# Router scores as 64 more columns of the z product, from a product of keys and Wq made once on the chip

## The chip, the cores and the metric

The kernel runs on one core of a Trainium2 chip. The metric is the device time of one execution in microseconds (us); the time before is 255.06 us, the median of three runs (254.93 to 255.38). The engines are TensorE (PE; its weight loads are PEld), VectorE (DVE), ScalarE (ACT), GpSimd (POOL) and SyncE (SP), which here issues nearly all transfers.

## The reference

For x of 32 x 64 x 1024, with J = 512 (64 experts of rank 8):

```
h    = conv1d(x, weight, 9 taps, 4 groups) + (cond @ c_weight.T)[:, :, None] + bias[None, :, None]
q    = h @ Wq.T                     # 1024 -> 16
s    = q @ keys.T                   # 16 -> 64 scores
gate = softmax over the 16 largest of s, 0 elsewhere
z    = (h @ A.T) gated, 8 columns for each expert      # 1024 -> 512
out  = x + 2 * (z @ B.T)            # 512 -> 1024
```

All is f32. A product of the kernel that has to be exact to nearly f32 is made from a rounded high half and a low half of each operand, in three passes: high x high, high x low, low x high. The halves have the type f32r (fp32r in the profile).

## The kernel before

The 2048 rows of 1024 are cut into 16 tiles (t or i) of 128 rows. A tile runs through these steps:

- **Convolution** (`conv`, L388): the tile's input, in blocks, is split by ScalarE (x_hi, `high` L253) and VectorE (x_lo, `low` L517); 2 groups of 6 matmuls of 512 columns each go to p_conv (tile 1: p_out). ScalarE adds the condition and the bias (`add_u`, L276, tile h_c), VectorE transposes in 32x32 blocks (`turn_h`, L534, h_t), and both split again (h_hi, h_lo).
- **z product** (`z_product`, L411): the stationary operand is a 128x128 chunk of h, the moving one a row block of A. A's 512 columns and Wq's 16 stand side by side in a_raw, a_hi and a_lo (JQ = 528) and are cut into two banks of HB = 264. So a tile has 8 chunks x 3 passes x 2 banks = 48 matmuls of 264 columns into p_z (tile 1: p_out). The last 16 columns of bank 1 are q.
- **Scores**: ScalarE copies q out (`take_q`, L306), TensorE turns it against the identity (`turn_q`, L422, f32, into p_q), ScalarE copies the turned q (`copy_q`, L310), TensorE multiplies it with the keys (`scores`, L426, a plain f32 matmul of 64 columns, two records in the profile), VectorE copies the scores (`copy_scores`, L559).
- **Gate**: VectorE finds the 16 largest (`choose`), ScalarE takes the exponential, VectorE makes e_top and the reciprocal of its sum (`weigh`, L582) and gates z (`gate`, L594, z_g, which frees the banks of p_z).
- **Output**: TensorE turns z_g (`turn_z`, L433, p_t), both engines split it (zt_hi, zt_lo), 24 matmuls of 512 columns make z @ B (`out_part`, L450 to L452), and VectorE adds x (`add`, L605). The last tile's second half is cut into two parts of 256 columns.

Every engine's order is written out by hand, and each engine runs its own in order; semaphores join them. TensorE's order: conditioning (4 matmuls, L460), convolutions of tiles 0 to 2, z of tile 0, convolution 3 (with turn_q(0) between its groups, scores(0) behind it), z of tile 1, z of tile 2 in pieces with the scores of 1 and 2 and turn_z(0) between them, convolution 4, turn_z(1), output of tile 0. From tile 3 on: z(i), with turn_q(i) in the middle of the second pass of bank 0, scores(i), convolution i+2, turn_z(i-1), output of tile i-2. Bank 1 comes before bank 0. The first z product of a tile waits for the gate of the tile before (L399 to L401).

At the start, ScalarE splits w and x of tiles 0 and 1, adds for tile 0, splits x of tile 2 and h of tile 0, and then the six chunks of A that are its own (a_hi; VectorE rounds chunks 5 and 7, L547, and makes every a_lo). ScalarE's queue issues one load, sm (conditioning, bias and keys); SyncE's queue has w, x of tiles 0 to 2, A, x of tile 3, B and the rest, in that order. GpSimd makes the constants, and later one x_lo, that of tile 4 (L247).

Of the kernel before, what the change touches and what calls it, by code (L numbers as in the profile page):

```python
# [6 lines left out]
ACT = mybir.ActivationFunctionType  # L7
# [3 lines left out]
P = 128  # L11
# [14 lines left out]
RD = 16  # L26
JQ = J + RD
HB = JQ // 2
E = 64
RANK = 8  # L30
JC = J // P
D = 128
SMALL_CW, SMALL_C, SMALL_B, SMALL_K = 0, 64, 96, 100
SMALL = 164


def adaln_ffn(nc, x_blocks, x_rows, conv_w, a_wq, b_w, small, out):

# [9 lines left out]
    with ExitStack() as ctx:  # L48
        def sb(name, shape, dt=F32):
            return ctx.enter_context(nc.sbuf_tensor(name, shape, dt))  # L50
# [4 lines left out]
        def sem(name):  # L55
            return ctx.enter_context(nc.semaphore(name))
# [14 lines left out]
        h_lo = sb("h_lo", [P, 2, R, P], F32R)  # L71
        a_raw = sb("a_raw", [P, R, JQ])
        a_hi = sb("a_hi", [P, R, JQ], F32R)
        a_lo = sb("a_lo", [P, R, JQ], F32R)
        b_raw = sb("b_raw", [P, JC, L])
# [7 lines left out]
        zt_lo = sb("zt_lo", [P, 2, JC, P], F32R)  # L83
        q_s = sb("q_s", [P, P])
        q_t = sb("q_t", [P, P])
        sc = sb("sc", [P, E])
# [14 lines left out]
        p_q = ps("p_q", [P, 512])  # L101
        QT, SC = slice(0, P), slice(P, P + E)

# [30 lines left out]
        s_z = sem("s_z")  # L134
        s_q = sem("s_q")
        s_qz = sem("s_qz")
        s_ahd = sem("s_ahd")
        s_qtp = sem("s_qtp")
        s_qt = sem("s_qt")
        s_scp = sem("s_scp")  # L140
        s_nm = sem("s_nm")
# [47 lines left out]
        @block.sync  # L189
        def _(sp):  # L190
            def load_blocks(t):
                if t >= XB:
                    sp.wait_ge(s_xhi, x_split_count(t - XB))
                    sp.wait_ge(*x_lo_done(t - XB))
                sp.dma_start(x_blk[:, t % XB], x_blocks[t]).then_inc(s_xb[t % XB], 16)

            def load_rows(t):
                if t >= XN:
                    sp.wait_ge(s_st[t % XN], 32 * (t // XN))
                sp.dma_start(x_nat[:, t % XN, :], x_rows[t]).then_inc(s_xn[t % XN], 16)  # L200
# [12 lines left out]
            for r in range(R):  # L213
                sp.dma_start(a_raw[:, r, :], a_wq[:, r]).then_inc(s_a[r], 16)
            load_blocks(3)
            for c in range(JC):
                sp.dma_start(b_raw[:, c, :], b_w[:, c]).then_inc(s_b[c], 16)
            load_blocks(4)
            sp.dma_start(w_raw[:, 1], conv_w[:, 1]).then_inc(s_w[1], 16)
            for t in range(XN):  # L220
                load_rows(t)
            for i in range(2, NT):
                if i + 3 < NT:
                    load_blocks(i + 3)
                store(i - 2)
                if 1 <= i - 2 and i + 1 < NT:
                    load_rows(i + 1)
            store(NT - 2)
            store(NT - 1)
            for k in range(XN):  # L230
                last = NT - XN + k
                sp.wait_ge(s_st[k], 32 * (last // XN) + 16 * len(parts(last)))

        @block.gpsimd
        def _(pool):
            nc.gpsimd.memset(ones[:], 1.0).then_inc(s_ones, 1)
            nc.gpsimd.memset(ident[:], 0.0).then_inc(s_iz, 1)
            nc.gpsimd.memset(q_s[:], 0.0).then_inc(s_qz, 1)
            pool.wait_ge(s_iz, 1)
# [11 lines left out]
        def _(act):  # L251
# [34 lines left out]
            def split_a(r):  # L286
                act.wait_ge(s_a[r], 16)
                high(a_hi[:, r, :], a_raw[:, r, :], s_ahi)

# [9 lines left out]

            def take_q(i):  # L300
                act.wait_ge(s_zq, i + 1)
                if i == 0:
                    act.wait_ge(s_qz, 1)
                if i >= 1:
                    act.wait_ge(s_qtp, i)
                nc.scalar.activation(q_s[:, 0:RD], z_bank(i, 1)[:, J - HB:HB], ACT.Copy).then_inc(s_q, 1)  # L306

            def copy_q(i):
                act.wait_ge(s_qtp, i + 1)
                nc.scalar.activation(q_t[:], p_q[:, QT], ACT.Copy).then_inc(s_qt, 1)  # L310

# [3 lines left out]

            act.dma_start(sm[:], small).then_inc(s_small, 16)
            split_w(0)
            split_x(0, 0)
# [5 lines left out]
            split_x(2)  # L324
            split_h(0)
            for r in A_ACT:
                split_a(r)
# [4 lines left out]
            add_u(2, 1)  # L332
            take_q(0)
            copy_q(0)
            split_h(1)
# [5 lines left out]
            split_h(2)  # L341
            take_q(1)
            split_b(1)
            copy_q(1)
            split_b(2)
            split_b(3)
            take_q(2)
            exp(1)
            split_z(0)
            copy_q(2)  # L350
            for i in range(2, NT):
                if i == 2:
                    split_h(3)
                else:
                    take_q(i)
                    copy_q(i)
                exp(i)
# [13 lines left out]
        def _(pe):  # L371
# [20 lines left out]
            def z_product(t, k, banks, chunks):  # L392
# [12 lines left out]
                for r in chunks:  # L405
                    if t == 0 and k == 0:
                        pe.wait_ge(*a_hi_done(r))
                    if t == 0 and k == 2:
                        pe.wait_ge(s_alo, r + 1)
                    for b in banks:  # L410
                        mm = nc.tensor.matmul(z_bank(t, b)[:, 0:HB], h[:, t % 2, r, :], a[:, r, b * HB:(b + 1) * HB],  # L411
                                              start=k == 0 and r == 0, stop=k == 2 and r == R - 1)
                        if k == 2 and r == R - 1:
                            mm.then_inc(s_zq if b else s_z, 1)

            def turn_q(i):
                pe.wait_ge(s_q, i + 1)
                if i >= 1:
                    pe.wait_ge(s_dve, STEPS * (i - 1) + 1)
                else:  # L420
                    pe.wait_ge(s_ident, 1)
                nc.tensor.transpose(p_q[:, QT], q_s[:], ident[:]).then_inc(s_qtp, 1)  # L422

            def scores(i):
                pe.wait_ge(s_qt, i + 1)
                nc.tensor.matmul(p_q[:, SC], q_t[:], sm[:, SMALL_K:SMALL_K + E], start=True, stop=True).then_inc(s_scp, 1)  # L426

# [35 lines left out]
            mm.then_inc(s_up, 1)  # L463
            for t in range(3):
                for g in range(NG):
                    conv(t, g)
            for k in range(3):
                z_product(0, k, (1, 0), range(R))
            conv(3, 0)
            turn_q(0)  # L470
            conv(3, 1)
            scores(0)
            for k in range(3):
                z_product(1, k, (1, 0), range(R))
            z_product(2, 0, (1,), range(R))
            turn_q(1)
            z_product(2, 1, (1,), range(R))
            scores(1)
            z_product(2, 2, (1,), range(R))
            turn_z(0)  # L480
            z_product(2, 0, (0,), range(R))
            z_product(2, 1, (0,), range(R // 2))
            turn_q(2)
            z_product(2, 1, (0,), range(R // 2, R))
            z_product(2, 2, (0,), range(R))
            scores(2)
            for g in range(NG):
# [4 lines left out]
            for i in range(3, NT):  # L492
# [3 lines left out]
                z_product(i, 1, (0,), range(R // 2))  # L496
                turn_q(i)
                z_product(i, 1, (0,), range(R // 2, R))
                z_product(i, 2, (0,), range(R))
                scores(i)  # L500
                if i + 2 < NT:
# [13 lines left out]
        def _(dve):  # L515
# [25 lines left out]
            def split_a(r):  # L541
                dve.wait_ge(*a_hi_done(r))
                low(a_lo[:, r, :], a_raw[:, r, :], a_hi[:, r, :], s_alo)

            def round_a(r):
                dve.wait_ge(s_a[r], 16)
                nc.vector.tensor_copy(a_hi[:, r, :], a_raw[:, r, :]).then_inc(s_ahd, 1)  # L547

# [8 lines left out]
            def copy_scores(i):  # L557
                dve.wait_ge(s_scp, i + 1)
                nc.vector.tensor_copy(sc[:], p_q[:, SC]).then_inc(s_dve, 1)  # L559

# [58 lines left out]
            split_x(2)  # L619
            split_h(0)  # L620
            split_a(0)
            round_a(5)
# [54 lines left out]
def laid_out(x, cond, bias, conv_w, cond_w, A_w, B_w, Wq_w, keys):  # L677
# [20 lines left out]

    a = np.concatenate([chunked(A_w), chunked(Wq_w)], axis=2)
    b = B_w.T.reshape(JC, P, L).transpose(1, 0, 2)  # L700
# [4 lines left out]
    small[:, SMALL_B:SMALL_B + 2 * NG] = np.tile(bias.reshape(2 * NG, CI).T, (R, 1))  # L705
    small[0:RD, SMALL_K:SMALL_K + E] = keys.T
    return {"x_blocks": x_blocks, "x_rows": x_rows, "conv_w": w, "a_wq": a, "b_w": b, "small": small}

# [21 lines left out]
```

## Time and profile before

| | |
|---|---|
| median of three runs | 255.06 us |
| the profiled execution | 253.84 us, of it a span of 252.0 us |
| TensorE busy | 246.4 us, 98% of the span |
| VectorE, ScalarE, GpSimd busy | 56%, 39%, 2% |
| granted clock of TensorE | 1.00 over the span |

The span runs from the first to the last instruction in the trace; the time of an execution holds some 1.8 us more. A matmul's length in the trace overlaps the next one's, so what it occupies is read from the distance of the starts.

### The profile page before, as it was taken

How to read it: one execution, taken by the hardware profiler on the slowest of the kernel's cores; microseconds unless marked ns; L12 is line 12 of the kernel's file. 1: busy time of each engine (PE TensorE's matmuls, PEld its weight loads, DVE VectorE, ACT ScalarE, POOL GpSimd, SP SyncE). 2: the span in 40 equal slices, each digit the busy share in tenths (PEclk: the TensorE clock that was granted, in tenths of full speed). 3: DMA queues.
4: the chain of work that ended last, by engine and by line, in shares of the span. 5: the costliest groups of instructions: out<-in, count | busy, mean ns of one | idle time of the engine just before them, and what ended most of it. 6: DMA issues, size and time to landing. Idle time of an engine off the chain costs nothing.

```text
span 252.0 us, 3991 instructions
## 1 busy us (share of the span) xinstructions
PE 246.4 (98%) x1492; PEld 218.6 (87%) x1492; DVE 141.4 (56%) x339; ACT 98.4 (39%) x239; POOL 4.0 (2%) x10
## 2 busy tenths in 40 slices
PE   7999899999999999999999999999999999999995
PEld 7689898898989889898998989889898988989885
DVE  1796989969175572827539173562817546151622
ACT  5896853635081531606135080532606133101100
POOL 2000300000000000000000000000000000000000
PEclk9999999999999999999999999999999999999999
DMA  7999400051604215070331605115070401313122
GB/s 218 383 409 406 196 4 0 0 170 41 209 3 140 110 54 201 0 246 8 126 124 42 211 0 188 65 70 181 3 250 1 134 35 43 127 42 125 54 103 97
DMA packets 11828, 30.37 MB, mean 120 GB/s; under 512 B 1312, under 2 KB 1696, under 8 KB 11808
## 3 DMA queue, kind: packets, MB, share of 16 engines
q1 hardware_dynamic: 11664, 30.02, 33.3%
q8 instruction: 12, 0.20, 0.3%
q10 hardware_dynamic: 144, 0.08, 0.2%
q14 instruction: 8, 0.07, 0.1%
HBM read 21.71 MB, written 8.39 MB: 119 GB/s over the span
## 4 chain that ended last, share of the span: by engine, by line
PE 90%; DVE 3%; DMA 2%; ACT 2%; issue 1%; SPq 1%; DVEq 0%; ACTq 0%
PE p_z L411 35%; PE p_conv L388 15%; PE p_out L452 12%; PE p_out L451 12%; PE p_out L450 12%; PE p_t L433 3%; DMA x_blk<-in_x_blocks 2%; PE p_q L426 1%; ACT h_c L276 1%; PE p_q L422 1%; DVE e_top L582 1%; DVE x_lo L517 0%; DVE h_lo L517 0%; ACT h_hi L253 0%; ACT x_hi L253 0%
## 5 line engine op out<-in xcount | busy, mean ns | idle before, releaser
L450 PE MATMUL p_out<-b_hi,zt_hi 128*128 128x512 f32 (+1 forms) x128 | 51.2, 400 | 0.0
L452 PE MATMUL p_out<-b_hi,zt_lo 128*128 128x512 f32 (+1 forms) x128 | 50.4, 393 | 0.0
L451 PE MATMUL p_out<-b_lo,zt_hi 128*128 128x512 f32 (+1 forms) x128 | 50.1, 391 | 0.0
L559 DVE COPY sc<-p_q 128x64 f32<-128x64 f32 x16 | 3.6, 224 | 66.7 <-PE p_q L426 66.7
L276 ACT ACTIVATE h_c<-p_conv,u 128x128 f32<-128x128 f32 x120 | 33.9, 380 | 6.2 <-PE p_conv L388 6.2
L411 PE MATMUL p_z<-a_hi,h_lo 128*128 128x264 f32 x240 | 35.6, 289 | 0.0
L411 PE MATMUL p_z<-a_hi,h_hi 128*128 128x264 f32 x240 | 34.3, 286 | 0.9 <-DVE z_g L594 0.9
L411 PEld LDWEIGHTS p_z<-a_hi,h_hi 128*128 128x128 f32 x240 | 32.2, 188 | 2.3 <-issue 1.1
L411 PE MATMUL p_z<-a_lo,h_hi 128*128 128x264 f32 x240 | 34.1, 284 | 0.0
L411 PEld LDWEIGHTS p_z<-a_hi,h_lo 128*128 128x128 f32 x240 | 31.9, 189 | 0.0
L411 PEld LDWEIGHTS p_z<-a_lo,h_hi 128*128 128x128 f32 x240 | 31.3, 188 | 0.0
L452 PEld LDWEIGHTS p_out<-b_hi,zt_lo 128*128 128x128 f32 x128 | 24.0, 188 | 5.5
L451 PEld LDWEIGHTS p_out<-b_lo,zt_hi 128*128 128x128 f32 x128 | 24.1, 188 | 5.2
L450 PEld LDWEIGHTS p_out<-b_hi,zt_hi 128*128 128x128 f32 x128 | 24.1, 188 | 5.0
L605 DVE SCALAR_TENSOR_TENSOR x_nat<-p_out,x_nat 128x512 f32<-128x512 f32 (+1 forms) x32 | 21.7, 679 | 11.5 <-PE p_out L452 11.0
L306 ACT ACTIVATE q_s<-p_z 128x16 f32<-128x16 f32 x15 | 2.8, 184 | 64.5 <-PE p_z L411 64.5
L534 DVE STREAM_TRANSPOSE h_t<-h_c 128x512 f32<-128x512 f32 x32 | 22.4, 706 | 4.9 <-ACT h_c L276 4.9
L517 DVE TENSOR_TENSOR h_lo<-h_t,h_hi 128x1024 fp32r<-128x1024 f32 x16 | 19.6, 1224 | 8.8 <-ACT h_hi L253 8.8
L517 DVE TENSOR_TENSOR x_lo<-x_blk,x_hi 128x1032 fp32r<-128x1032 f32 (+1 forms) x17 | 18.7, 1100 | 6.3 <-ACT x_hi L253 6.3
L388 PE MATMUL p_conv<-x_hi,w_hi 128*128 128x512 f32 x60 | 20.2, 418 | 0.0
L253 ACT ACTIVATE h_hi<-h_t 128x1024 fp32r<-128x1024 f32 x16 | 17.0, 1064 | 7.7 <-DVE h_t L534 7.7
L388 PE MATMUL p_conv<-x_lo,w_hi 128*128 128x512 f32 x60 | 19.1, 400 | 0.5 <-DVE x_lo L517 0.5
(71 smaller groups left out, 238.5 us busy)
## 6 DMA issues: line engine op xcount, KB each, us to landing
x_nat<-in_x_rows SPq DMA_DIRECT2D x16, 512.0 KB, 4.0
out_dram<-x_nat SPq DMA_DIRECT2D x31, 256.0 KB, 2.1
x_blk<-in_x_blocks SPq DMA_DIRECT2D x14, 516.0 KB, 4.7
a_raw<-in_a_wq SPq DMA_DIRECT2D x8, 264.0 KB, 7.2
b_raw<-in_b_w SPq DMA_DIRECT2D x4, 512.0 KB, 9.8
x_blk<-in_x_blocks SPq DMA_DIRECT2D x4, 258.0 KB, 4.2
w_raw<-in_conv_w SPq DMA_DIRECT2D x2, 256.0 KB, 8.0
out_dram<-x_nat SPq DMA_DIRECT2D x2, 128.0 KB, 1.7
```

Of the source, the lines that this page charges most:

```text
L253: nc.scalar.activation(dst, src, ACT.Copy).then_inc(s, 1)
L276: last = nc.scalar.activation(h_c[:, t % 2, g, n, :], conv_bank(t, g)[:, n * LB:(n + 1) * LB], ACT.Identity, bias=u[:, t // 8 * NG + g, at ...
L388: mm = nc.tensor.matmul(bank, w[:, pair, s, g, :], x[:, t % 2, g, :, s:s + LB], start=k == 0 and s == 0, stop=k == 2 and s == 1)
L411: mm = nc.tensor.matmul(z_bank(t, b)[:, 0:HB], h[:, t % 2, r, :], a[:, r, b * HB:(b + 1) * HB], start=k == 0 and r == 0, stop=k == 2 and r ...
L433: mm = nc.tensor.transpose(p_t[:, c * P:(c + 1) * P], z_g[:, t % 2, c * P:(c + 1) * P], ident[:])
L450: nc.tensor.matmul(dst, zt_hi[:, t % 2, c, :], b_hi[:, c, cols], start=c == 0, stop=False)
L451: nc.tensor.matmul(dst, zt_hi[:, t % 2, c, :], b_lo[:, c, cols], start=False, stop=False)
L452: mm = nc.tensor.matmul(dst, zt_lo[:, t % 2, c, :], b_hi[:, c, cols], start=False, stop=c == JC - 1)
L517: nc.vector.tensor_tensor(dst, src, hi.bitcast(F32), ALU.subtract).then_inc(s, 1)
L534: nc.vector.transpose(h_rows[:, :, :, g, :], h_c[:, t % 2, g].rearrange("q n (k c) -> q n k c", c=CI)).then_inc(s_tr, 1)
L559: nc.vector.tensor_copy(sc[:], p_q[:, SC]).then_inc(s_dve, 1)
L605: nc.vector.scalar_tensor_tensor(out=x_nat[:, t % XN, lo:hi], in0=src, scalar=SCALING, in1=x_nat[:, t % XN, lo:hi], op0=ALU.mult, op1=ALU. ...
```

## The change

Wq and keys are joined on the chip, once: an own load brings wk (16 x 1088: Wq's columns in the order of A's chunks, then keys turned), and 8 plain f32 matmuls of 64 columns make keys x Wq, chunk by chunk, into p_q. ScalarE and VectorE split that as high and low halves into 64 more columns of a_hi and a_lo. The z product's columns grow from 528 to 576 (banks of 288), and its last 64 columns are the scores; the 16 for q are gone. `take_q`, `turn_q`, `copy_q` and `scores` are gone in every tile, and so are q_s, q_t and GpSimd's fill of q_s; `copy_scores` reads p_z once bank 1 is complete. TensorE makes the keys product between the convolutions of tiles 0 and 1; both splits stand ahead of the splits of A on their engines. a_raw has 512 columns.

```diff
-JQ = J + RD
-HB = JQ // 2
+JE = J + E
+HB = JE // 2
@@ ScalarE
-                high(a_hi[:, r, :], a_raw[:, r, :], s_ahi)
+                high(a_hi[:, r, 0:J], a_raw[:, r, :], s_ahi)
-            def take_q(i):
...
-            def copy_q(i):
...
+            def split_wk():
+                act.wait_ge(s_wkp, 1)
+                high(a_hi[:, :, J:JE], p_q[:].rearrange("p (r e) -> p r e", r=R), s_wkhi)
             act.dma_start(sm[:], small).then_inc(s_small, 16)
+            act.dma_start(wk[:], wq_keys).then_inc(s_wk, 16)
...
             split_h(0)
+            split_wk()
             for r in A_ACT:
                 split_a(r)
@@ TensorE
                     if t == 0 and k == 0:
                         pe.wait_ge(*a_hi_done(r))
+                    if t == 0 and k == 0 and r == 0:
+                        pe.wait_ge(s_wkhi, 1)
+                    if t == 0 and k == 2 and r == 0:
+                        pe.wait_ge(s_wklo, 1)
...
-            for t in range(3):
+            for g in range(NG):
+                conv(0, g)
+            pe.wait_ge(s_wk, 16)
+            for r in range(R):
+                mm = nc.tensor.matmul(p_q[:, r * E:(r + 1) * E], wk[:, r * P:(r + 1) * P], wk[:, L:L + E], start=True, stop=True)
+            mm.then_inc(s_wkp, 1)
+            for t in range(1, 3):
                 for g in range(NG):
                     conv(t, g)
...
                 z_product(i, 1, (0,), range(R // 2))
-                turn_q(i)
                 z_product(i, 1, (0,), range(R // 2, R))
                 z_product(i, 2, (0,), range(R))
-                scores(i)
@@ VectorE
+            def split_wk():
+                dve.wait_ge(s_wkhi, 1)
+                low(a_lo[:, :, J:JE], p_q[:].rearrange("p (r e) -> p r e", r=R), a_hi[:, :, J:JE], s_wklo)
             def copy_scores(i):
-                dve.wait_ge(s_scp, i + 1)
-                nc.vector.tensor_copy(sc[:], p_q[:, SC]).then_inc(s_dve, 1)
+                dve.wait_ge(s_zq, i + 1)
+                nc.vector.tensor_copy(sc[:], z_bank(i, 1)[:, J - HB:HB]).then_inc(s_dve, 1)
...
             split_h(0)
+            split_wk()
             split_a(0)
```

## Rows read from the trace of the kernel before

**Rows 1.** The page's first part: busy us (share of the span) x instructions.
```profile
PE 246.4 (98%) x1492; PEld 218.6 (87%) x1492; DVE 141.4 (56%) x339; ACT 98.4 (39%) x239; POOL 4.0 (2%) x10
```

**Rows 2.** The page's chain that ended last, by engine.
```profile
PE 90%; DVE 3%; DMA 2%; ACT 2%; issue 1%; SPq 1%; DVEq 0%; ACTq 0%
```

**Rows 3.** The waits of TensorE: us in total, times, longest.
```profile
PE p_z L411 <- DVE z_g L594: 0.9, 1, 0.9
...
PE p_conv L388 <- DVE x_lo L517: 0.5, 1, 0.5
```

**Rows 4.** Windows of PE: stretch, busy (matmuls), granted clock, DMA, GB/s.
```profile
15.50:21.35 5.85, 5.85 (x49) 1.00 1.02 405
...
107.63:116.64 9.01, 9.01 (x64) 1.00 0.50 173
...
107.63:122.67 15.04, 15.04 (x92) 1.00 0.31 107
246.31:249.07 2.76, 2.76 (x24) 1.00 0.25 95
```

**Rows 5.** PE in order of time (start, us, what), convolution of tile 3, first group.
```profile
21.36 0.64 PE L388 MATMUL p_conv<-x_hi,w_hi 128*128 128x512 f32 x2
...
22.78 0.27 PE L422 MATMUL p_q<-ident,q_s 128*128 128x128 f32 x1
```

**Rows 6.** PE in order of time, the last output matmuls.
```profile
238.16 0.40 PE L451 MATMUL p_out<-b_lo,zt_hi 128*128 128x512 f32 x1
...
246.32 0.28 PE L450 MATMUL p_out<-b_hi,zt_hi 128*128 128x256 f32 x1
```

**Rows 7.** PE in order of time, turn and scores of a steady tile.
```profile
112.03 0.27 PE L422 MATMUL p_q<-ident,q_s 128*128 128x128 f32 x1
112.06 0.74 PE L411 MATMUL p_z<-a_hi,h_lo 128*128 128x264 f32 x4
...
113.61 0.33 PE L426 MATMUL p_q<-sm,q_t 128*128 128x64 f32 x2
113.75 0.71 PE L388 MATMUL p_conv<-x_hi,w_hi 128*128 128x512 f32 x2
114.30 0.63 PE L388 MATMUL p_conv<-x_hi,w_lo 128*128 128x512 f32 x2
```

**Rows 8.** PE in order of time, the start.
```profile
5.14 1.08 PE L460 MATMUL p_t<-sm,cw 128*128 128x32 f32 x8 [0.52 <-POOL cw L243]
...
8.99 0.63 PE L388 MATMUL p_out<-x_hi,w_hi 128*128 128x512 f32 x2
...
11.81 0.71 PE L388 MATMUL p_conv<-x_hi,w_hi 128*128 128x512 f32 x2
```

**Rows 9.** DMA issues of the first 20 us: KB each, median us to landing.
```profile
sm<-in_small ACTq DMA_DIRECT2D x1, 82.0 KB, 3.7
```

**Rows 10.** Groups by line: busy us, mean ns, idle before.
```profile
L517 DVE TENSOR_TENSOR zt_lo<-p_t,zt_hi 128x512 fp32r<-128x512 f32 x16 | 10.6, 659 | 0.4 <-ACT zt_hi L253 0.4
L253 ACT ACTIVATE zt_hi<-p_t 128x512 fp32r<-128x512 f32 x16 | 9.8, 611 | 4.9 <-PE p_t L433 4.8
```

**Rows 11.** ScalarE and VectorE in order of time, the splits of A.
```profile
12.52 3.35 ACT L253 ACTIVATE a_hi<-a_raw 128x528 fp32r<-128x528 f32 x6
...
15.97 3.80 DVE L517 TENSOR_TENSOR a_lo<-a_raw,a_hi 128x528 fp32r<-128x528 f32 x6
```

**Rows 12.** In order of time: the z product of tile 2 and its releasers; a steady e_top.
```profile
27.69 2.43 POOL L247 TENSOR_TENSOR x_lo<-x_blk,x_hi 128x1032 fp32r<-128x1032 f32 x1 [22.61 <-ACT x_hi L253]
...
28.40 1.80 DVE L582 SCALAR_TENSOR_TENSOR e_top<-sc_b,e_all 128x64 f32<-128x64 f32 x1
...
30.45 0.88 DVE L594 SCALAR_TENSOR_TENSOR z_g<-p_z,e_inv,e_top 128x248 f32<-128x248 f32 x2
31.24 1.22 DVE L517 TENSOR_TENSOR h_lo<-h_t,h_hi 128x1024 fp32r<-128x1024 f32 x1
...
31.47 1.22 PE L411 MATMUL p_z<-a_hi,h_hi 128*128 128x264 f32 x8 [0.93 <-DVE z_g L594]
...
115.80 0.23 DVE L582 SCALAR_TENSOR_TENSOR e_top<-sc_b,e_all 128x64 f32<-128x64 f32 x1
```

More of the change, by code:

```diff
@@ L32, with adaln_ffn @@
 D = 128
-SMALL_CW, SMALL_C, SMALL_B, SMALL_K = 0, 64, 96, 100
-SMALL = 164
-def adaln_ffn(nc, x_blocks, x_rows, conv_w, a_wq, b_w, small, out):
+SMALL_CW, SMALL_C, SMALL_B = 0, 64, 96
+SMALL = 100
+def adaln_ffn(nc, x_blocks, x_rows, conv_w, a_w, wq_keys, b_w, small, out):
     with ExitStack() as ctx:
@@ L71, in adaln_ffn @@
         h_lo = sb("h_lo", [P, 2, R, P], F32R)
-        a_raw = sb("a_raw", [P, R, JQ])
-        a_hi = sb("a_hi", [P, R, JQ], F32R)
-        a_lo = sb("a_lo", [P, R, JQ], F32R)
+        a_raw = sb("a_raw", [P, R, J])
+        wk = sb("wk", [RD, L + E])
+        a_hi = sb("a_hi", [P, R, JE], F32R)
+        a_lo = sb("a_lo", [P, R, JE], F32R)
         b_raw = sb("b_raw", [P, JC, L])
@@ L83, in adaln_ffn @@
         zt_lo = sb("zt_lo", [P, 2, JC, P], F32R)
-        q_s = sb("q_s", [P, P])
-        q_t = sb("q_t", [P, P])
         sc = sb("sc", [P, E])
@@ L101, in adaln_ffn @@
         p_q = ps("p_q", [P, 512])
-        QT, SC = slice(0, P), slice(P, P + E)
         s_ones = sem("s_ones")
@@ L134, in adaln_ffn @@
         s_z = sem("s_z")
-        s_q = sem("s_q")
-        s_qz = sem("s_qz")
+        s_wk = sem("s_wk")
+        s_wkp = sem("s_wkp")
+        s_wkhi = sem("s_wkhi")
+        s_wklo = sem("s_wklo")
         s_ahd = sem("s_ahd")
-        s_qtp = sem("s_qtp")
-        s_qt = sem("s_qt")
-        s_scp = sem("s_scp")
         s_nm = sem("s_nm")
@@ L213, in _ @@
             for r in range(R):
-                sp.dma_start(a_raw[:, r, :], a_wq[:, r]).then_inc(s_a[r], 16)
+                sp.dma_start(a_raw[:, r, :], a_w[:, r]).then_inc(s_a[r], 16)
             load_blocks(3)
@@ L237, in _ @@
             nc.gpsimd.memset(ident[:], 0.0).then_inc(s_iz, 1)
-            nc.gpsimd.memset(q_s[:], 0.0).then_inc(s_qz, 1)
             pool.wait_ge(s_iz, 1)
@@ L298, in split_z @@
                 high(zt_hi[:, t % 2], p_t[:].rearrange("j (c t) -> j c t", c=JC), s_zthi)
-            def take_q(i):
[L301 to L306, printed above, removed]
-            def copy_q(i):
-                act.wait_ge(s_qtp, i + 1)
-                nc.scalar.activation(q_t[:], p_q[:, QT], ACT.Copy).then_inc(s_qt, 1)
+            def split_wk():
+                act.wait_ge(s_wkp, 1)
+                high(a_hi[:, :, J:JE], p_q[:].rearrange("p (r e) -> p r e", r=R), s_wkhi)
             def exp(i):
@@ L332, in _ @@
             add_u(2, 1)
-            take_q(0)
-            copy_q(0)
             split_h(1)
@@ L341, in _ @@
             split_h(2)
-            take_q(1)
             split_b(1)
-            copy_q(1)
             split_b(2)
             split_b(3)
-            take_q(2)
             exp(1)
             split_z(0)
-            copy_q(2)
             for i in range(2, NT):
@@ L353, in _ @@
                     split_h(3)
-                else:
-                    take_q(i)
-                    copy_q(i)
                 exp(i)
@@ L414, in z_product @@
                             mm.then_inc(s_zq if b else s_z, 1)
[L416 to L426, printed above, removed]
             def turn_z(t):
@@ L469, in _ @@
             conv(3, 0)
-            turn_q(0)
             conv(3, 1)
-            scores(0)
             for k in range(3):
@@ L475, in _ @@
             z_product(2, 0, (1,), range(R))
-            turn_q(1)
             z_product(2, 1, (1,), range(R))
-            scores(1)
             z_product(2, 2, (1,), range(R))
@@ L482, in _ @@
             z_product(2, 1, (0,), range(R // 2))
-            turn_q(2)
             z_product(2, 1, (0,), range(R // 2, R))
             z_product(2, 2, (0,), range(R))
-            scores(2)
             for g in range(NG):
@@ L542, in split_a @@
                 dve.wait_ge(*a_hi_done(r))
-                low(a_lo[:, r, :], a_raw[:, r, :], a_hi[:, r, :], s_alo)
+                low(a_lo[:, r, 0:J], a_raw[:, r, :], a_hi[:, r, 0:J], s_alo)
+            def split_wk():
+                dve.wait_ge(s_wkhi, 1)
+                low(a_lo[:, :, J:JE], p_q[:].rearrange("p (r e) -> p r e", r=R), a_hi[:, :, J:JE], s_wklo)
             def round_a(r):
                 dve.wait_ge(s_a[r], 16)
-                nc.vector.tensor_copy(a_hi[:, r, :], a_raw[:, r, :]).then_inc(s_ahd, 1)
+                nc.vector.tensor_copy(a_hi[:, r, 0:J], a_raw[:, r, :]).then_inc(s_ahd, 1)
             def split_b(c):
@@ L697, in chunked @@
         return m.reshape(-1, 4, 32, 2, 4).transpose(4, 2, 1, 3, 0).reshape(P, R, -1)
-    a = np.concatenate([chunked(A_w), chunked(Wq_w)], axis=2)
+    wk = np.concatenate([Wq_w.reshape(RD, 4, 32, 2, 4).transpose(0, 1, 3, 4, 2).reshape(RD, L), keys.T], axis=1)
     b = B_w.T.reshape(JC, P, L).transpose(1, 0, 2)
@@ L705, in laid_out @@
     small[:, SMALL_B:SMALL_B + 2 * NG] = np.tile(bias.reshape(2 * NG, CI).T, (R, 1))
-    small[0:RD, SMALL_K:SMALL_K + E] = keys.T
-    return {"x_blocks": x_blocks, "x_rows": x_rows, "conv_w": w, "a_wq": a, "b_w": b, "small": small}
+    return {"x_blocks": x_blocks, "x_rows": x_rows, "conv_w": w, "a_w": chunked(A_w), "wq_keys": wk, "b_w": b, "small": small}
 _INS = ["x", "cond_128", "fside_S_0", "L0_cond_weight", "L0_cond_c_weight", "L0_ffn_A_w", "L0_ffn_B_w",
```

## The prediction

> **What bounds the kernel now.** I read the page's shares first, then the chain of waits, the waits of TensorE, its order of time at four places, and last the windows. TensorE is busy for 98% of the span; VectorE and ScalarE have more than a third of it free [rows 1]. The chain that ended last runs 90% through TensorE [rows 2]. TensorE waits for another engine for only two stretches worth a look once it has started: 0.9 us for the gated z of tile 0, and 0.5 us (0.52) for the low half of x of tile 2 [rows 3]. A steady tile, from z product to z product, takes 15.04 us, all of it busy, at a granted clock of 1.00 [rows 4]. So the end moves by what TensorE's instruction stream gains or loses, less what falls into those two waits. What the change takes off ScalarE and VectorE (two copies a tile, the wait for the scores) is idle time of engines that are not the bound, and I count it at nothing; TensorE's stream covers it.
>
> **Part 1, the z product grows from 528 to 576 columns.** Each of its matmuls streams 288 columns in place of 264. There are 48 a tile (8 chunks, 3 passes, 2 banks), 768 in all. Three spacings bear on the price. At 264 columns the 48 matmuls of tile 0, with nothing between them, take 5.85 us [rows 4]: 121.9 ns each. At 512 columns, starts 238.16 and 246.32 lie 35 matmuls apart [rows 6]: 233.1 ns. At 256 columns the 24 matmuls of the tail have starts 2.76 us apart from first to last [rows 4, 6]: 120.0 ns. From 264 to 512 that is 0.448 ns a column, from 256 to 512 it is 0.442; the 2.4 GHz of the granted clock alone would be 0.417, 10.0 ns for 24 columns. From 256 to 264 it is only 1.9 ns in 8 columns, 0.24 each, 5.7 ns for 24. Upward, the line through 256 and 512, drawn to 288, gives 134.1 ns, 12.2 more than now. I take 10.6 ns (the slope over the long distance, which two pairs of rows give alike): 768 x 10.6 = **+8.1 us**, with ends +4.4 (5.7 ns) and +9.4 (12.2 ns). The weight loads do not set the spacing: the two passes of the scores matmul, each with a weight load of its own, start 0.14 us apart as a pair, 0.07 us each [rows 7], far under 0.12.
>
> **Part 2, the turn of q and the scores matmul go, 16 of each.** Their lengths (0.27 and 0.33 us) are not their price, since matmuls overlap: the turn starts at 112.03 and the next z matmul at 112.06 [rows 7]. The price is how much longer the stretch is. Window 107.63 to 116.64, one tile's z product, turn, scores and two groups of convolutions, takes 9.01 us [rows 4]. Without turn and scores it would be 5.85 us for the 48 z matmuls plus 12 convolution matmuls; six of these, after a z product and with nothing in between, take from 21.36 to 22.78 [rows 5], 1.42, so twelve take 2.84. 9.01 - 5.85 - 2.84 = 0.32 us a tile. x16 = **-5.1 us**. Ends: 0.28 and 0.36 a tile for the rounding of the starts, -4.5 and -5.8.
>
> The Trainium skill (TensorE: Matmul & The Clock Gate, Part 4: PE-mode transpose) says that a 128x128 transpose takes about 275 ns in a kernel's context. The trace's own length agrees (0.27 us [rows 7]), yet as a price it would be 2.5 us too much over 16 turns: with the skill's figure the sum below would end at 0.0 instead of +2.5. It is among the rivals as a mechanism.
>
> **Part 3, the product of keys and Wq.** Eight matmuls of 64 columns in plain f32 (16 rows deep, 128 weight columns) are put between the convolutions of tiles 0 and 1, that is at 8.99 us [rows 8]. The nearest row is the scores matmul, the same kind and width: 0.14 us for its pair of passes, and the first two convolution matmuls behind it take 0.55 in place of 0.47 [rows 7]. 8 x 0.14 + 0.08 = **+1.2 us**. Upper bound: the four matmuls of the conditioning, 8 records in 1.08 us [rows 8], which doubles to 2.2 for 16; lower bound 0.9, if a pass of depth 16 were as cheap as its share of columns. They need wk on the chip. It is the second issue of ScalarE's queue; the first, 82 KB, landed 3.7 us after its issue [rows 9], near 4.5 us. For 70 KB behind it I expect some 5 us, with 4 us to spare before 8.99. In a busy stretch of the DMA queues it takes 70 KB / 0.4 MB per us, 0.17 us, from the loads of w and x of tiles 0 and 1, while a_raw loses 64 KB later: **+0.1 us**, ends 0 and 0.3.
>
> ScalarE's and VectorE's new splits (128x512 out of PSUM) are like those of zt: 0.61 and 0.66 us [rows 10]. They stand ahead of the splits of A. On ScalarE, behind the new wait for the keys product (done near 10.3) are the six a_hi, 12.52 to 15.87 [rows 11]; the wait is over when ScalarE gets there, so they move 0.6 later, less 0.1 for 512 columns in place of 528. The sixth (chunk 6) ends near 16.4 and TensorE asks for it near 17.5. VectorE's a_lo end at 19.77 now [rows 11], then near 20.3; the last is asked for near 22. Both splits cost nothing on the path; without that cover they would cost their 0.6 each.
>
> **Part 4, the two waits.** From 11.81, the first convolution matmul of tile 2, to the start of the z product at 15.51 TensorE takes 3.70 us [rows 4, 8] for work that takes 2.84: 0.86 us go to the wait for x_lo of tile 2. x_lo hangs on ScalarE and VectorE and not on the convolution of tile 1, so it doesn't move with the 1.2 us put in: TensorE arrives that much later, after x_lo is done. **-0.86 us**, so the start ends 0.34 later.
> At the z product of tile 2 (31.47) TensorE has waited 0.93 us for z_g of tile 0 [rows 12], that is since 30.54. It would now be there at 30.54 + 0.34 + 0.1 + 2 x 0.51 (wider z, tiles 0 and 1) - 0.32 (turn and scores of tile 0) = 31.7. The releaser does not hang on that stream: e_top waited at 28.40 for 1.80 us, while GpSimd's x_lo ran from 27.69 to 30.12, and z_g followed at 30.45 to 31.33 [rows 12]. The low half of x of tile 4 moves by 0.1 at most (it follows ScalarE's copies behind convolution 3, now near 25.3 for the second group), and losing the wait for the turned q gives VectorE a second back. So z_g is ready by 31.4, before TensorE: **-0.93 us**, ends -0.5 and -0.93. Late next is h_lo of tile 2, behind z_g (31.24 to 32.46 now [rows 12]), for which TensorE asks one pass later, near 32.75: 0.2 to spare, or 0.1 to 0.3 lost.
>
> The Trainium skill (SBUF — State Buffer, the bullets on the shared port pair) holds that a VectorE instruction with two SBUF inputs and a GpSimd instruction that reads SBUF exclude each other for a whole instruction. The 1.80 us of e_top, 0.23 in a steady tile [rows 12], ended just as GpSimd's ended; by that rule a weigh step that starts before GpSimd's would release z_g some 2 us earlier. The sum stays, as TensorE comes after either.
>
> **Sum.** +8.1 - 5.1 + 1.2 + 0.1 - 0.86 - 0.93 = +2.5 us. By tiles: +0.2 at the z product of tile 2, then 14 x 0.51 for columns, less 15 x 0.32. The profiled execution took 253.84 us (span 252.0 and 1.8 around it), so it would be 256.4; on the median of 255.06 it is **257.6 us**. The steady tile goes from 15.04 to 15.04 + 0.51 - 0.32 = 15.23 us.
>
> **Rivals.**
> - *The columns are nearly free* (the other side): if the spacing near 264 columns is set by a fixed cost of each matmul, the widening costs little. For it: 8 columns more cost 1.9 ns from 256 to 264. Against it: 512 columns cost 111 ns more, and the passes of the scores are 0.07 us apart, so no such floor shows at that size. At 5.7 ns a matmul: 8.1 becomes 4.4, sum -1.2, 253.9 us. At 0 ns: sum -5.6 + 0.9 (the wait at tile 2 stays) = -4.7, 250.4 us. It decides from under 7.3 ns a matmul, where the sum is zero.
> - *Turn and scores cost their length.* 16 x (0.27 + 0.33) = 9.6 in place of 5.1: sum -2.0, 253.1 us. Against it: the starts beside the turn, 0.03 us apart, and the window.
> - *The start pays more.* wk lands late, or its passes cost as the conditioning's do (+1.0), or z_g or h_lo of tile 2 are late and a wait stays (+0.3 to +0.9): 258.4 to 259.8 us. For it: that queue lies beside loads that keep the DMA engines busy, and the spare of h_lo is 0.2. Against it: the 4 us to spare of wk.
> - *It doesn't do what it says*: the wider z product of a steady tile could come to wait for the gate of the tile before. But its release is not late now (no such wait after tile 2 is among TensorE's waits [rows 3]), and the scores become ready a bank earlier, the time of 24 z matmuls; I give it no chance of its own.
>
> **How the numbers follow.** Forecast 0.72 (its own range 256.0 to 258.8, from the ends of part 1 above 8 ns and of part 2); columns nearly free 0.12; cost by length 0.04; a dearer start 0.12. The range of 255.8 to 259.0 leaves out most of the second and third and the worst of the last. What can be told from no change is 0.2%, 0.5 us. Faster by more: 0.10 of the free columns and 0.04 = 0.14. Within: 0.04 from the edges of forecast and free columns. Slower: 0.82.
>
> **What would show it.** Right: z matmuls 132 to 133 ns apart, a steady tile of 15.2 us, no wait of TensorE at the z product of tile 2, and none for x_lo of tile 2; eight keys matmuls in 1.2 us near 9 us; the z product of tile 0 starting near 15.9. Wrong: z spacing at 128 ns or under (the first rival), a steady tile under 14.9 with z at 132 (the second), or a wait above 0.3 us before 35 us (the third).

## The result and the profile after

The changed kernel takes 260.02 us (median of 4 executions, 259.12 to 261.51), the kernel before 255.00 beside it: ratio 1.0216 (95% interval 1.015 to 1.0282). It is five us slower, where +2.5 was forecast; 260.02 lies above the forecast's range, which ended at 259.0. The profiled execution took 259.12 us, with a span of 257.1.

The first part of the page (as [rows 1]), and the chain of waits by engine (as [rows 2]):

```profile
PE 253.4 (99%) x1460; PEld 225.5 (88%) x1460; DVE 140.9 (55%) x340; ACT 92.1 (36%) x208; POOL 3.9 (2%) x9
...
PE 99%; DVE 0%; issue 0%; POOL 0%; POOLq 0%
```

TensorE still sets the end, now without a break: the only wait that is left is the one for the first constant. Both waits of [rows 3] are gone. TensorE's waits, all of them:

```profile
PE p_q L431 <- POOL ones L234: 1.0, 1, 1.0
```

Windows of TensorE over two steady tiles, then the z product of one, then its convolutions (columns as in [rows 4]):

```profile
50.21:65.43 15.22, 15.22 (x89) 1.00 0.21 73
65.43:80.66 15.23, 15.23 (x89) 1.00 0.30 105
50.21:56.56 6.35, 6.35 (x49) 1.00 0.35 111
56.57:59.40 2.83, 2.83 (x14) 1.00 0.33 128
```

The steady tile is the 15.23 us of the forecast, and the z matmuls are 6.35 / 48 = 132.4 ns apart. So the missing 2.5 us are not there. They are at the start. TensorE in order of time:

```profile
4.76 1.92 PE L434 MATMUL p_t<-sm,cw 128*128 128x32 f32 x8
6.48 1.20 PE L370 MATMUL p_conv<-x_hi,w_hi 128*128 128x512 f32 x2
7.48 1.05 PE L370 MATMUL p_conv<-x_lo,w_hi 128*128 128x512 f32 x2
8.34 1.05 PE L370 MATMUL p_conv<-x_hi,w_lo 128*128 128x512 f32 x2
...
11.23 1.99 PE L442 MATMUL p_q<-wk 16*128 16x64 f32 x16
13.15 0.73 PE L370 MATMUL p_out<-x_hi,w_hi 128*128 128x512 f32 x2
13.72 0.64 PE L370 MATMUL p_out<-x_lo,w_hi 128*128 128x512 f32 x2
14.20 0.64 PE L370 MATMUL p_out<-x_hi,w_lo 128*128 128x512 f32 x2
...
18.93 2.28 PE L397 MATMUL p_z<-a_hi,h_hi 128*128 128x288 f32 x16
```

From 7.48 to 8.34 two matmuls of 512 columns take 0.86 us, about 430 ns each (427 over a longer row of them): the clock's lower level (512 columns at 1.2 GHz), not its higher one (235 ns apart before). The clock rose later than in the trace before, which has the higher level from its first convolution on; this is called a late rise below. The convolutions of tile 0 run from 6.48 to 11.23, 4.75 us, where [rows 8] has them end at 8.99. The keys product takes 1.92 us, the convolutions behind it follow at the higher level (13.72 to 14.20, 240 ns each), and the z product starts at 18.93 instead of 15.50. (In this trace no record of the clock exists, so its windows print 1.00; the spacings tell the level. In other traces, too, 1.00 is printed for the time before the first record, so a mean of 1.00 does not exclude a late rise.)

A fact about the measurement is needed for what follows: single executions of either kernel fall into two groups about 2 us apart. Of 23 of the kernel before on one chip, 12 lay at 253.0 to 253.8 and 11 at 255.1 to 256.6.

### The profile page after: what moved, and what is told of

Read it like the earlier page. It is cut to its first block, busy times and chain, and to the rows that moved or that the text cites. A ratio compares the mean times of both kernels' runs of the same rounds, so it can differ in the third digit from the quotient of the medians.

```text
span 257.1 us, 3866 instructions
## 1 busy us (share of the span) xinstructions
PE 253.4 (99%) x1460; PEld 225.5 (88%) x1460; DVE 140.9 (55%) x340; ACT 92.1 (36%) x208; POOL 3.9 (2%) x9
## 4 chain that ended last, share of the span: by engine, by line
PE 99%; DVE 0%; issue 0%; POOL 0%; POOLq 0%
PE p_z L397 37%; PE p_conv L370 17%; PE p_out L424 11%; PE p_out L426 11%; PE p_out L425 11%; PE p_t L407 3%; PE p_out L397 2%; PE p_q L431 1%; PE p_out L370 1%; PE p_q L442 1%; PE p_t L434 1%; PE p_z L426 0%; PE p_z L424 0%; PE p_z L425 0%; DVE x_nat L581 0%
## 5 line engine op out<-in xcount | busy, mean ns | idle before, releaser
L397 PE MATMUL p_z<-a_hi,h_hi 128*128 128x288 f32 x240 | 36.6, 295 | 0.0
L397 PE MATMUL p_z<-a_lo,h_hi 128*128 128x288 f32 x240 | 36.5, 294 | 0.0
L397 PE MATMUL p_z<-a_hi,h_lo 128*128 128x288 f32 x240 | 36.5, 294 | 0.0
L397 PEld LDWEIGHTS p_z<-a_hi,h_hi 128*128 128x128 f32 x240 | 34.2, 188 | 1.2
L303 ACT ACTIVATE e_all<-sc,neg_max 128x64 f32<-128x64 f32 x16 | 5.6, 350 | 82.8 <-DVE neg_max L548 82.8
L397 PEld LDWEIGHTS p_z<-a_hi,h_lo 128*128 128x128 f32 x240 | 33.4, 188 | 0.0
L397 PEld LDWEIGHTS p_z<-a_lo,h_hi 128*128 128x128 f32 x240 | 33.4, 188 | 0.0
L535 DVE COPY sc<-p_z 128x64 f32<-128x64 f32 x15 | 3.3, 223 | 29.6 <-PE p_z L397 29.6
## 6 DMA issues: line engine op xcount, KB each, us to landing
out_dram<-x_nat SPq DMA_DIRECT2D x31, 256.0 KB, 2.2
a_raw<-in_a_w SPq DMA_DIRECT2D x8, 256.0 KB, 7.1
w_raw<-in_conv_w SPq DMA_DIRECT2D x2, 256.0 KB, 7.7
```

The source lines that it names most:

```text
L303: nc.scalar.activation(e_all[:], sc[:], ACT.Exp, bias=neg_max[:]).then_inc(s_e, 1)
```

## The experiments

Each ran beside the kernel before on the same chip; groups are given where there are two. Three chips were used, and before's two groups have medians of 253.3 and 255.3 to 255.5 on all of them. Theory A blames a clock that comes late because of the change, B chance alone; D and E, later, are about which sort of matmuls make the clock fall.

**e1 and e2, both kernels again**, no edit.

> The changed kernel again, unaltered. In its first trace twelve convolution matmuls of tile 0 began at 6.48 us and ran until 11.23 (427 ns apart at first, later 235); in the kernel before they began at 6.05 and ran until 8.99. Theory A (the change causes the late rise of TensorE's clock): the trace again has 427 ns spacings until about 10 us, the z product of tile 0 starts near 18.9, and the ratio to before is 1.020 to 1.022. Theory B (the moment of the rise is chance from execution to execution): another trace may have the rise near 4.3 us, with the z product starting near 16.6 and a span of about 254.9, and the ratio is anything from 1.011 to 1.022.

> The kernel before again, unaltered, with a trace of its own. Theory A: rise of the clock near 4.3 us, the z product of tile 0 starts at 15.5, span 252.0, ratio 1.000. Theory B: the rise may come late here too, with 427 ns spacings of the convolution matmuls, the z product of tile 0 near 17.3 and a span near 253.3; ratio 1.000 in any case.

e1: ratio 1.0202 (1.0148 to 1.0257), median 259.55: 258.42 to 259.03 in three executions, 260.07 to 260.45 in three. e2: 0.9995 (0.9953 to 1.0036), z product at 15.52. The loss repeats in both groups: medians 258.47 against before's 253.3, 260.3 against 255.5, that is +5.2 and +4.8. Of A the ratio came out, but not the place: the late rise is not there in e1's profiled execution (lower group, 258.47 us), so it comes and goes as B has it. In its stead there is another stretch of low clock:

```profile
5.99 0.71 PE L370 MATMUL p_conv<-x_hi,w_hi 128*128 128x512 f32 x2
...
9.23 1.99 PE L442 MATMUL p_q<-wk 16*128 16x64 f32 x16
11.16 0.74 PE L370 MATMUL p_out<-x_hi,w_hi 128*128 128x512 f32 x2
11.73 0.75 PE L370 MATMUL p_out<-x_lo,w_hi 128*128 128x512 f32 x2
12.28 1.06 PE L370 MATMUL p_out<-x_hi,w_lo 128*128 128x512 f32 x2
13.13 1.06 PE L370 MATMUL p_out<-x_hi,w_hi 128*128 128x512 f32 x2
...
18.47 2.28 PE L397 MATMUL p_z<-a_hi,h_hi 128*128 128x288 f32 x16
```

Its windows, third column the granted clock:

```profile
9.00:11.00 2.00, 2.00 (x18) 1.00 1.00 363
11.00:12.00 1.00, 1.00 (x7) 1.00 1.06 397
12.20:15.40 3.20, 3.20 (x9) 0.50 1.05 412
15.60:18.40 2.80, 2.80 (x13) 1.00 1.03 410
```

TensorE is busy throughout, yet behind the keys product the clock is at half; this is called a fall below. It lowers the mean granted clock of the execution to 0.993. All three executions of e1's lower group have that mean, and one of its upper group.

**e3, the keys product twice.**

```diff
-            for r in range(R):
-                mm = nc.tensor.matmul(p_q[:, r * E:(r + 1) * E], ...
+            for _ in range(2):
+                for r in range(R):
+                    mm = nc.tensor.matmul(p_q[:, r * E:(r + 1) * E], ...
```

> The keys product is made twice (32 matmul passes in place of 16), all else as changed. If a pass costs 0.12 us, as its spacing in the trace of the changed kernel shows: +1.9 us on the changed kernel. If it costs 0.07 us, as forecast from the scores matmul: +1.1 us. If the stretch is partly hidden behind a wait that it displaces: under +1 us.

261.83 us, 2.3 over e1 (ratio to before 1.0312, 1.0251 to 1.0373): 0.12 us a pass, not 0.07, and a little more of the low clock (mean granted clock 0.987 in four of six, 0.993 and 0.980 in the others). In its profiled execution, the worst at 264.06, the clock fell twice, and the first time ahead of the keys product, behind the conditioning matmuls (in order of time, then windows with the granted clock as third column):

```profile
5.65 1.08 PE L434 MATMUL p_t<-sm,cw 128*128 128x32 f32 x8 [1.05 <-POOL cw L240]
6.67 0.71 PE L370 MATMUL p_conv<-x_hi,w_hi 128*128 128x512 f32 x2
...
8.04 1.10 PE L370 MATMUL p_conv<-x_hi,w_lo 128*128 128x512 f32 x2
...
11.42 4.29 PE L443 MATMUL p_q<-wk 16*128 16x64 f32 x32
15.64 1.22 PE L370 MATMUL p_out<-x_hi,w_hi 128*128 128x512 f32 x2
```

```profile
9.00:11.00 2.00, 2.00 (x6) 0.50 1.00 371
11.00:12.00 1.00, 1.00 (x7) 0.95 1.05 395
15.60:18.40 2.80, 2.80 (x8) 0.50 1.02 407
```

So a fall of this size can come without the keys product.

**e4, no keys product.** The opening matmuls fill the bank that is split.

```diff
-            for _ in range(8):
-                nc.tensor.matmul(p_q[:, 0:P], ones[:], ones[:], start=True, stop=True)
+            for k in range(8):
+                mm = nc.tensor.matmul(p_q[:, k % 4 * P:(k % 4 + 1) * P], ones[:], ones[:], start=True, stop=True)
+            mm.then_inc(s_wkp, 1)
...
-            for r in range(R):
-                mm = nc.tensor.matmul(p_q[:, r * E:(r + 1) * E], wk[:, r * P:(r + 1) * P], wk[:, L:L + E], start=True, stop=True)
-            mm.then_inc(s_wkp, 1)
```

> The keys product is left out (the eight opening matmuls fill the bank that is split in its place, so the scores are those of another matrix); the load of wk, its splits and the 288 columns stay. Without its 1.92 us the wait for x_lo of tile 2 comes back. With a clock that rises as late as in the changed kernel (theory A, if what causes it is not the product): about -1.9 us on the changed kernel, as ScalarE's copies behind the late convolution of tile 0 still come later. With a rise near 4.3 us: -3.5 us or more, 256.0 or less.

256.45 us (1.0076, 1.0036 to 1.0116), groups 255.1 to 255.8 and 257.2 to 258.4: +2.0 and +1.7 on before's. Without the product the kernel costs what the steady tiles cost. So the product alone is worth 3.1 us in either group, of which its passes are 1.9. None of the six executions of the lower group shows a fall. But two of the upper group (257.16 and 257.17 us) have a mean granted clock of 0.993, that of a fall, though no keys product runs in them; where it lay is not known, since the execution that was profiled (258.43 us) has a late rise and no fall.

**e5, the same passes, 128 rows deep.**

```diff
-        wk = sb("wk", [RD, L + E])
+        wk = sb("wk", [P, L + E])
+            nc.vector.memset(wk[:], 0.0).then_inc(s_wkz, 1)
+            act.wait_ge(s_wkz, 1)
-            act.dma_start(wk[:], wq_keys).then_inc(s_wk, 16)
+            act.dma_start(wk[0:RD], wq_keys).then_inc(s_wk, 16)
```

> The keys product as before in 16 passes of 64 columns, but 128 rows deep in place of 16 (112 rows of zeros, filled by VectorE before the load). Theory D (the shallow product, with 112 of 128 array rows unused, is what makes TensorE's clock fall to its lower level for 3.4 us behind it): no fall, and 1.3 to 1.6 us less than the changed kernel where that has the fall, 0 where it has a late rise instead. Rival E (the time that a narrow plain f32 pass leaves the array idle does it, whatever the depth): the fall stays, same time as the changed kernel. On a pass's price: if depth 16 makes it 0.12 us, the passes now take 0.07 each and 0.8 us go; if each plain f32 pass with its own weight load takes 0.11 to 0.12 in a row, as the four conditioning matmuls do, they stay at 1.8 to 1.9 us.

256.87 us (1.0105, 1.0055 to 1.0156): four executions at 256.0 to 256.9, two at 258.4 and 258.8, 1.5 to 2.4 under the medians of e1's groups. No execution has a mean granted clock under 0.998, and the trace (256.88 us) has no fall:

```profile
9.29 1.89 PE L444 MATMUL p_q<-wk 128*128 128x64 f32 x16
10.99 0.71 PE L372 MATMUL p_out<-x_hi,w_hi 128*128 128x512 f32 x2
11.54 0.63 PE L372 MATMUL p_out<-x_lo,w_hi 128*128 128x512 f32 x2
...
16.73 2.28 PE L399 MATMUL p_z<-a_hi,h_hi 128*128 128x288 f32 x16
```

The passes barely changed, 1.70 us in place of 1.92, so a row of plain f32 passes costs 0.11 to 0.12 us each at both depths. On the clock this is what D expected, and not E. It is not a clean test of D: the wait for the zeros also held up ScalarE's first splits, and TensorE stood idle for 0.40 us ahead of the product (waiting for x_hi), which it does not in e1.

**e6, one matmul with a block diagonal of keys.**

```diff
-            for r in range(R):
-                mm = nc.tensor.matmul(p_q[:, r * E:(r + 1) * E], wk[:, r * P:(r + 1) * P], wk[:, L:L + E], start=True, stop=True)
+            pe.wait_ge(s_kd, 2)
+            mm = nc.tensor.matmul(p_q[:], wk[:, 0:P], kd[:].rearrange("p r e -> p (r e)"), start=True, stop=True)
```

> The keys product as ONE plain f32 matmul of 512 columns and 128 rows: chunk r of Wq on partitions 16r to 16r+15, keys in a block diagonal that GpSimd makes from a repeated copy. Two passes at 2 array cycles a column: 0.85 us plus 0.1, in place of 1.92. If the dense matmul also spares the fall of the clock: 2.5 us less than the changed kernel in its quicker executions, near 255.9; if the fall stays: 1.0 us less. The wait for x_lo of tile 2 may come back by a few tenths.

257.25 us (1.0083, 1.005 to 1.0116), groups 255.8 to 256.1 and 257.2 to 257.6: 2.6 and 2.9 under e1's, as expected without a fall; no execution has a mean granted clock under 0.999. This is the best form of the change, still 2.5 and 1.9 over before's two groups.

**e7, columns back to 264, turn, scores and keys product left out** (e4 with `JE = J + RD`, and the splits and the copy of the scores cut down to fit).

> The z product has its 264 columns again, keys product, turn of q and scores matmul are all left out (the last 64 columns of z stand for the scores, and 16 columns split from the opening matmuls' bank for q): the kernel before without parts 2 and 3's TensorE work, or e4 without part 1. If 24 columns cost 10.5 ns a matmul: 8.1 us under e4, less up to 0.9 if the wait for z_g of tile 2 comes back, so 248.3 to 249.2; a steady tile 14.72 us. If turn and scores cost what their length says (0.60 a tile): 14.44.

249.42 us (0.9783, 0.9736 to 0.9831); lower group 247.8 to 248.0, 7.5 under e4's, with a wait of 0.4 us for z_g back, as expected (7.2 to 8.1). Here, too, with no keys product, two of the four other executions (249.55 and 249.68 us) have a mean granted clock of 0.993 and 0.991. The windows over two tiles:

```profile
60.46:75.17 14.71, 14.71 (x89) 1.00 0.31 107
75.17:89.88 14.71, 14.71 (x89) 1.00 0.33 108
```

So 24 columns cost 15.225 - 14.71 = 0.51 us a tile, 10.7 ns a matmul. Before's tiles take 15.04 and 15.09 in turn (starts of the z products), 15.065 on the mean: turn and scores cost 15.065 - 14.71 = 0.35.

**e8, before with a denser opening**, and **e12**, the same with 10 opening matmuls and the conditioning behind conv(0, 1).

```diff
-            for _ in range(8):
+            for _ in range(11):
                 nc.tensor.matmul(p_q[:, 0:P], ones[:], ones[:], start=True, stop=True)
+            conv(0, 0)
             pe.wait_ge(s_cw, 1)
...
-            for t in range(3):
+            conv(0, 1)
+            for t in range(1, 3):
```

> The kernel before with 11 opening matmuls in place of 8, and the conditioning matmuls behind the first group of convolutions of tile 0, so that TensorE is dense until the convolutions. The kernel before has two groups of times, near 253.3 and 255.4. If these are an early and a late rise of TensorE's clock at the start, the slower group goes or shrinks: times 253.2 to 254.2 throughout, the median 0 to 1 us lower. If the groups have another cause, both stay.

> The kernel before with 10 opening matmuls and the conditioning matmuls behind both convolution groups of tile 0. In e8 the opening ended at 5.8 and held the convolutions up by 0.3 us, and the conditioning stood within them. One group of times if the dense opening is what joins them; 253.5 to 254.2 if what e8 lost to before's quicker group was that hold-up, 254.4 as e8 if it was the conditioning's place in the stream or the later rise.

e8: one group, 253.97 to 254.67, median 254.42 (1.0001, 0.9971 to 1.0032). It joins the two groups between them. e12: one group too, 255.32 to 255.87 (1.0063, 1.0031 to 1.0095), but higher: TensorE waited for x_lo of tiles 1 and 2 (0.43 and 0.53 us), and the z product of tile 0 began at 17.32, where e8 has 16.01. That u (the condition, from the late conditioning matmuls) held ScalarE's copies up is the likely reason, and it isn't shown. So e12 does not tell where e8 lost its 1 us to before's lower group, and neither beats that group.

**e9, e6 with e8's opening.**

> The keys product as one block-diagonal matmul (as e6), together with the denser opening of e8 (11 opening matmuls, conditioning behind the first convolution group). e6 had two groups of times, 255.8 and 257.4; e8 had one, near 254.4, where before has 253.3 and 255.5. If the late rise of the clock makes e6's upper group, it goes: times of 256.4 to 257.0 in one group, that is e8 plus the steady tiles' 2.1 and the product's 0.2 to 0.5. If it stays in two groups, the opening is not what they come from.

256.69 us (1.01, 1.0048 to 1.0152), one group, 256.48 to 256.93, as expected.

**e10, e11, e14, the kernel before again**, one profiled execution each.

> The kernel before, once more, for a trace of one of its slower executions (9 and 11 of 23 lay near 255.4). If such an execution has a span of 253.4 or more: 427 ns spacings of the convolution matmuls from about 6.5 us to 10, no fall later, and the z product of tile 0 near 17.2 in place of 15.5. If the span is near 251.6: spacings of 235 ns from the start.

All three fell into the lower group (253.36, 253.40, 253.69 us), so no trace of before's upper group exists. (Of the 23 executions beside e5 to e8 eleven lay in each group, not nine in the upper one, and one took 622.62 us.) In e11 the z product starts at 15.06.

**e13, before with 2 opening matmuls.**

```diff
-            for _ in range(8):
+            for _ in range(2):
```

> The kernel before with 2 opening matmuls in place of 8. If the upper group of times of the kernel before (255.4) is a late rise of TensorE's clock, taking most of the opening away makes the rise late always: one group near 255.4, convolution matmuls 427 ns apart from about 6 us, and a clock at its higher level from about 10 us. If the groups come from something else, two groups 2 us apart stay.

One group, 255.07 to 256.31, median 255.83 (1.0047, 1.0012 to 1.0082), 0.5 over before's upper group (median 255.3 beside it). Its start:

```profile
6.34 1.20 PE L388 MATMUL p_conv<-x_hi,w_hi 128*128 128x512 f32 x2
7.34 1.05 PE L388 MATMUL p_conv<-x_lo,w_hi 128*128 128x512 f32 x2
...
17.45 2.12 PE L411 MATMUL p_z<-a_hi,h_hi 128*128 128x264 f32 x16
```

A late rise costs before 2.4 us here: the z product starts at 17.45 in place of 15.06. That before's own upper group is made of late rises is likely by this, and not shown by a trace.

**e15 and e16, the changed kernel again**, one profiled execution each (260.32 and 259.90 us, both of the upper group).

> The changed kernel, one look. With a span near 256.7: as the repeat, a fall behind the keys product and the z product of tile 0 at 18.5. With a span near 258.4: either a late rise and a fall behind the keys product as well, or a keys product that runs wholly at the lower level; the z product of tile 0 near 20.2 in both.

e15 has the convolutions of tile 0 wholly at the lower level (6.84 to 12.23) and the keys product at 2.17 us, and no fall behind it: the next convolutions follow at 240 ns. e16 has both troubles, a late rise and then a fall:

```profile
7.32 1.05 PE L370 MATMUL p_conv<-x_lo,w_hi 128*128 128x512 f32 x2
...
10.15 0.63 PE L370 MATMUL p_conv<-x_hi,w_lo 128*128 128x512 f32 x2
10.71 1.99 PE L442 MATMUL p_q<-wk 16*128 16x64 f32 x16
12.63 1.06 PE L370 MATMUL p_out<-x_hi,w_hi 128*128 128x512 f32 x2
13.49 1.05 PE L370 MATMUL p_out<-x_lo,w_hi 128*128 128x512 f32 x2
...
19.92 1.34 PE L397 MATMUL p_z<-a_hi,h_hi 128*128 128x288 f32 x9
```

## Why the prediction was wrong

The direction and the steady part were right; the start was off by 3.0 us. Term by term, for e1's profiled execution (span 256.68) against e11's (251.60), both of the lower groups:

| term | forecast | measured |
|---|---|---|
| columns, 16 tiles | +8.1 | +8.2 (e7: 0.51 a tile) |
| turn and scores | -5.1 | -5.6 (e7: 0.35 a tile) |
| keys product | +1.2 | +1.9 |
| loads, start of convolutions | +0.1 | -0.1 (5.99 against 6.07) |
| convolutions of tile 0, small waits | 0 | +0.4 |
| clock at half behind the product | not in the sum | +1.7 |
| wait for x_lo of tile 2 | -0.86 | -0.5 (all there is in e11's trace) |
| wait for z_g of tile 2 | -0.93 | -0.9 |
| sum | +2.5 | +5.1 |

*The failed step is part 3*, "8 x 0.14 + 0.08 = +1.2 us", and what was not written beside it. I took the price of a pass from a lone pair of scores passes, between matmuls of another kind, 0.07 each. The row that fitted was the one used as the upper bound, the four conditioning matmuls in a row [rows 8]: such passes, each with its weight load, follow at 0.11 to 0.12. That is 0.7 us (e3, e5). That a lone pair hides part of its time behind its neighbours, and a row of them can't, would explain the difference; no run tests it.

*The larger part is the clock.* The sum used the higher level for all of TensorE's stream, since [rows 4] and the whole page show 1.00. But in e1 the convolutions behind the product ran at 427 ns for 3.4 us: 1.7 us. That the product brings this fall in the lower group rests on four things. It stands right behind the product, in e1 and e16. Leaving the product out (e4) gives back 3.1 us, 1.2 more than its passes. All three executions of e1's lower group have the mean clock of a fall, and none of the 15 in the lower groups of e4, e5 and e6, nor any of the 74 executions of the kernel before that ran beside e1 to e16 (one of 622.62 us left out). Passes of equal number and nearly equal length, 128 rows deep, give 1.5 to 2.4 us less (e5), one dense matmul 2.6 (e6).

Against a plain rule there are three facts. The product can run without a fall behind it: the first trace of the changed kernel and e15 have none, and only seven of the kernel's twelve executions have the mean clock of one. The fall can come without the product: ahead of it in e3's trace, and in four of the 18 executions of e4 and e7. And both traces with a product and no fall have a late rise, but so has e16, which has the fall. So the shallow passes make a fall more likely here; what else decides it, and whether depth is what counts, stays open. The Trainium skill (TensorE: Matmul & The Clock Gate, Part 1) makes the return to 1.2 GHz a matter of an idle engine; in e1 TensorE was busy without a break from 4.91 us until the fall near 12, so the measurement decides: busy time alone did not hold the level.

In the upper groups the terms are different. Both traces of the changed kernel there (e15, e16) have a late rise, and e13 stands in for the kernel before. Its z product starts at 17.45; e15 and e16 have 20.17 and 19.92, 2.7 and 2.5 later. The first trace of the changed kernel (259.12 us, between the groups) has a late rise that ended sooner and no fall: 18.93, 1.5 later. Against e13, e15 starts 0.5 later, has 0.4 more on the convolutions of tile 0, and 2.2 for the product. Why an execution gets the late rise is not shown: kernel and opening are the same in both groups. The prediction did not know of the groups: the profiled execution that it was worked out from (253.84 us) is of the lower one, and the three times of its median (254.93 to 255.38) are of the upper one.

*The steady tile's 15.23 us is partly luck.* The tile of 15.04 us it was worked out from is the shorter of the two that take turns, and turn and scores cost 0.35, not 0.32: two errors of 0.03 that cancel in one tile.

*Part 4 held, with room to spare.* z_g came before TensorE needed it. After, in order of time on VectorE and GpSimd:

```profile
29.84 0.23 DVE L558 SCALAR_TENSOR_TENSOR e_top<-sc_b,e_all 128x64 f32<-128x64 f32 x1 [0.30 <-ACT e_all L303]
...
30.76 2.43 POOL L244 TENSOR_TENSOR x_lo<-x_blk,x_hi 128x1032 fp32r<-128x1032 f32 x1 [26.06 <-ACT x_hi L250]
...
32.60 1.67 DVE L489 TENSOR_TENSOR h_lo<-h_t,h_hi 128x1024 fp32r<-128x1024 f32 x1 [1.42 <-ACT h_hi L250]
```

e_top starts ahead of GpSimd's x_lo and takes 0.23 us, not the 1.80 of [rows 12]. So z_g was ready at 31.18 in this trace, and TensorE came to it at 34.52; in e5, where the start is less late, at 28.97 and 32.31. The forecast had put the two 0.3 us apart (31.4 and 31.7), with x_lo moving by 0.1 at most; it moved by 1.3 (27.25 in e11, 28.55 in e5), which did no harm behind e_top. h_lo, issued when x_lo had 0.59 us left to run, takes 1.67 in place of 1.22. The Trainium skill (SBUF — State Buffer, SBUF: two separate sides) has the second of such a pair wait until the first is done; the trace agrees in kind, with 0.45 us added.

*The rivals.* Free columns: refuted, 10.7 ns a matmul; the 0.24 ns a column between 256 and 264 was no slope to build on. Cost by length: refuted, 0.35 a tile against 0.60. The dearer start was the right one in kind, at 258.4 to 259.8, but of its reasons only the price of the passes came true; wk landed 4.1 us after its issue, at 5.3, in good time.

## What to carry to other kernels

Price a change of TensorE's stream by distances of starts in a stretch of the same make-up: the lone pair of passes here was 0.07 us a pass, the row of them 0.12. And where a small product of few rows is put into a dense stream, look at the clock behind it, not only at its own length: here 1.9 us of work was followed, in about half of the executions, by a fall of the clock that cost 1.7 us. Packed as one full matmul (e6) it brought no fall and cost 0.2 to 0.5 us over the kernel without the product (e4, on another chip), yet the change stays a loss, because 24 more columns in 48 matmuls (0.51 us) outweigh one turn and one small matmul (0.35 us) in every tile.

## What the runs showed of the hardware

- TensorE's clock fell from its higher to its lower level while TensorE had no idle time, behind 16 passes 16 rows deep (e1, e16), and stayed up behind the same passes in two other traces (the first after, e15) and behind 16 passes 128 rows deep in e5's. In e3 it also fell behind eight passes of 32 columns, 128 rows deep, that had followed 1.05 us of idle time.
- Executions of one kernel form two groups about 2 us apart. Of the changed kernel, both traces of the upper group (e15, e16) have a late first rise of the clock and e1's, of the lower group, has not; the first trace, between the groups, has one. For the kernel before this is inferred from e13. Filling the stretch before the convolutions with dense matmuls (e8, e9) left one group.
- Few rows saved next to nothing: a weight load of 16 rows took a median of 187 ns, one of 128 rows 192 (e1, e5), and the passes 0.12 and 0.11 us.
- f32r matmuls of 256, 264, 288 and 512 columns followed each other at 120, 122, 132 and 233 ns.
